# Second graph layer: message sums over five PSUM banks, and rows weighed by an SBUF copy of the weights

## What is computed

```python
    edge_index = jnp.stack([src, dst])
    x = _layernorm(x + _L0_gnn_ref(x, edge_index, L0_gnn_w0, L0_gnn_w1), axis=-1)
    x = _layernorm(x + _L1_gnn_ref(x, L1_gnn_W, L1_gnn_attn_src, L1_gnn_attn_dst, edge_index, edge_type_8), axis=-1)
```

```python
        h_src = h_all[edge_type, src]
        h_dst = h_all[edge_type, dst]
        scores = jnp.einsum('ehd,hd->eh', h_src, attn_src) + jnp.einsum('ehd,hd->eh', h_dst, attn_dst)
        scores = jnp.where(scores > 0, scores, NEG_SLOPE * scores)
        amax = jnp.maximum(jax.ops.segment_max(scores, dst, num_segments=n), 0.0)
        w = jnp.exp(scores - amax[dst])
        denom = jax.ops.segment_sum(w, dst, num_segments=n) + 1e-12
        w = w / denom[dst]
        msg = h_src * w[..., None]
        out = jax.ops.segment_sum(msg, dst, num_segments=n)
```

## Time and profile before

| What | us |
|---|---|
| Timed runs, median of 3 (lowest to highest) | 2754.34 (2751.61 to 2757.78) |
| Profiled execution: span from its first to its last instruction | 3067.8 |
| Busy in it: TensorE matmuls / weight loads | 2357.8 / 1676.6 |
| Busy in it: VectorE / ScalarE / POOL | 1943.7 / 1618.7 / 1840.7 |

### The profile page before, as it was taken

How to read it: one execution, slowest core, us unless ns; L and a number is a source line. 1 busy time by engine, 2 the same in 40 slices (tenths; PEclk the granted TensorE clock), 3 DMA queues, 4 the chain that set the end, 5 groups by cost and what they waited for, 6 DMA issues and landing times.

```text
span 3067.8 us, 38107 instructions
## 1 busy us (share of the span) xinstructions
PE 2357.8 (77%) x9936; PEld 1676.6 (55%) x9936; DVE 1943.7 (63%) x4273; ACT 1618.7 (53%) x3465; POOL 1840.7 (60%) x1875
## 2 busy tenths in 40 slices
PE   8786688899999989999981667766776667766675
PEld 3455566666666666666651545444554555554541
DVE  9893656554555555545530767767777777677787
ACT  4573455655555555555540555555655555455543
POOL 1004766677777767776617566666666666666625
PEclk9897899999999999999985777878878788687788
DMA  5103446644444444444533444444444444444424
GB/s 155 49 13 113 123 122 161 211 146 143 146 136 142 141 146 142 144 141 144 135 138 105 107 128 120 122 123 117 133 121 120 122 120 124 118 130 122 118 69 142
DMA packets 177777, 387.53 MB, mean 126 GB/s; under 512 B 42669, under 2 KB 106867, under 8 KB 171042
## 3 DMA queue, kind: packets, MB, share of 16 engines
q0 software_dynamic: 83888, 233.09, 28.3%
q1 hardware_dynamic: 86626, 99.05, 10.6%
q10 hardware_dynamic: 7056, 52.99, 4.5%
HBM read 302.96 MB, written 82.03 MB: 125 GB/s over the span
## 4 chain that ended last, share of the span: by engine, by line
PE 51%; DVE 18%; issue 15%; another core or an unknown queue 8%; ACT 3%; DVEq 2%; POOL 1%; DMA 1%; SPq 0%; ACTq 0%; POOLq 0%
PE ps L1695 22%; PE ps L1811 11%; PE ps L1745 10%; DVE nodes L895 6%; PE ps L1794 3%; DVE nodes L777 2%; DVE region L884 2%; PE ps L1664 1%; ACT region L1461 1%; PE ps L1652 1%; DVE edge_z L1029 1%; DVEq L895 1%; ACT region L1465 1%; DVE region L868 1%
## 5 line engine op out<-in xcount | busy, mean ns | idle before, releaser
L1303 POOL DMA_INDIRECT region<-y_d,edge_z x856 | 875.0, 1022 | 571.4 <-issue 231.4
L1348 POOL DMA_INDIRECT region<-ha_d,idx_t x880 | 891.7, 1013 | 495.3 <-issue 242.7
L777 DVE TENSOR_TENSOR nodes<-ps,nodes 128x512 f32 x856 | 591.8, 691 | 616.0 <-PE ps L1695 333.2
L1695 PE MATMUL ps<-region 128*128 128x256 f32 x3424 | 830.1, 394 | 134.7 <-issue 72.8
L1811 PE MATMUL ps<-region 128*128 128x264 f32 x1760 | 645.0, 502 | 279.5 <-DVE nodes L895 114.1
L1695 PEld LDWEIGHTS ps<-region 128*128 128x128 f32 x3424 | 654.2, 196 | 343.4 <-issue 207.3
L1811 PEld LDWEIGHTS ps<-region 128*128 128x128 f32 x1760 | 370.2, 237 | 467.1 <-issue 177.8
L895 DVE TENSOR_TENSOR nodes<-ps,nodes 128x264 f32 x880 | 374.0, 425 | 304.6 <-remote 207.1
L1461 ACT ACTIVATE region<-iota_n,edge_z 128x256 f32<-128x256 f32 x856 | 364.7, 500 | 62.7 <-PE ps L1695 40.3
L1745 PE MATMUL ps<-region,edge_z 128*128 128x512 f32 x784 | 366.8, 598 | 12.5 <-ACT edge_z L1491 7.5
L1503 ACT COPY region<-ps 128x512 f32<-128x512 f32 x196 | 114.2, 586 | 403.2 <-PE ps L1745 169.5
(11 more groups left out here) (265 smaller groups left out, 1826.8 us busy)
## 6 DMA issues: line engine op xcount, KB each, us to landing
ha_d<-region ACTq DMA_DIRECT2D x49, 1056.0 KB
region<-near_d SPq DMA_DIRECT2D x55, 512.0 KB
region<-ha_d,idx_t POOLq DMA_INDIRECT x880
region<-y_d,edge_z POOLq DMA_INDIRECT x856
edge_z<-level_d SPq DMA_DIRECT2D x55, 136.0 KB
kl_d<-region SPq DMA_DIRECT2D x8, 903.0 KB
edge_z<-kl_d SPq DMA_DIRECT2D x55, 129.0 KB
y_d<-edge_z SPq DMA_DIRECT2D x25, 256.0 KB, 3.2
```

Source lines behind the costliest of these rows:

```text
L777: v.tensor_tensor(into, ps[:, u, :], into, ALU.add).then_inc(added0, 1)
L1303: g.indirect_dma_start(rows0[c % RING][:, u, :], None, y_d, bass.IndirectOffsetOnAxis(ap=y_idx[:, k:k + 1], axis=0), bounds_check=node_bou ...
L1348: g.indirect_dma_start(rows[s][:, k, :], None, ha_rows, bass.IndirectOffsetOnAxis(ap=idx_t[:, B * b + k:B * b + k + 1], axis=0), bounds_ch ...
L1695: mm = t.matmul(ps[:, u, h * D:(h + 1) * D], lhsT=sel0[c % SEL][:, u, h * P:(h + 1) * P], rhs=rows0[c % RING][:, u, :], start=True, stop=True)
```

## The change

The sums of the second layer go round five banks, 0 to 4, by the step's number in the whole layer, so that a matmul waits for the add five steps earlier. Bank 4 is free for that since the turned weights now go to columns 128 to 255 of bank 7, beside the scores (columns 0 to 127) and the levels (256 to 511). As the banks must not be written by one engine while another reads them, the copy of the turned weights is made at once, before the factor's operand, and the transpose of the scores into bank 7 waits for it; on TensorE it now stands behind the last quarter of the sums of batch `i - 2`. The rows are multiplied by the copy in SBUF, which is in the last 8 columns of the same rows. The first sum of a batch no longer waits for the copy by a semaphore of its own. The factor row goes to the bank of the batch's first step.

```diff
+    SLOT = 5
...
-            w_turn = ps[:, 4, 0:P].rearrange("p (k h) -> p k h", k=B)
+            w_turn = ps[:, 7, P:2 * P].rearrange("p (k h) -> p k h", k=B)
 
             def weigh(b, q):
                 s = b % 4
                 if q == 0:
-                    v.wait_ge(w_turned, b + 1)
+                    v.wait_ge(w_ready, b + 1)
                 v.tensor_tensor(rows[s][:, 4 * q:4 * q + 4, 0:D].rearrange("p u (h d) -> p u h d", h=H),
                                 rows[s][:, 4 * q:4 * q + 4, 0:D].rearrange("p u (h d) -> p u h d", h=H),
-                                w_turn[:, 4 * q:4 * q + 4, :].unsqueeze(3).to_broadcast([P, 4, H, HD]),
+                                rows[s][:, 4 * q:4 * q + 4, D:AW].unsqueeze(3).to_broadcast([P, 4, H, HD]),
                                 ALU.mult).then_inc(msgs, 1)
...
-                v.tensor_tensor(acc[:, ds(tile * AW, AW)], ps[:, u, 0:AW], acc[:, ds(tile * AW, AW)],
+                v.tensor_tensor(acc[:, ds(tile * AW, AW)], ps[:, at % SLOT, 0:AW], acc[:, ds(tile * AW, AW)],
                                 ALU.add).then_inc(added, 1)
...
-                by = ps[:, 0, AW:AW + H]
+                by = ps[:, B * b % SLOT, AW:AW + H]
...
                 if a:
+                    v.wait_ge(w_turned, i)
+                    v.tensor_copy(rows[(i - 1) % 4][:, :, D:AW], w_turn).then_inc(w_ready, 1)
                     v.wait_ge(factors, i)
                     v.tensor_scalar(fm, factor, 1.0, ident[:, 0:1], ALU.subtract, ALU.mult).then_inc(fm_made, 1)
...
                 if a:
                     weigh(i - 1, 0)
-                    v.tensor_copy(rows[(i - 1) % 4][:, :, D:AW], w_turn).then_inc(w_ready, 1)
...
             def factor_rows(b):
                 t.wait_ge(fm_made, b + 1)
                 t.wait_ge(sel_made, 4 * b + 1)
-                t.wait_ge(added, B * b + 1)
-                t.matmul(ps[:, 0, AW:AW + H], lhsT=sel[0][:, 0, :], rhs=fm, start=True, stop=True).then_inc(fm_ps, 1)
+                if b:
+                    t.wait_ge(added, B * b - SLOT + 5)
+                t.matmul(ps[:, B * b % SLOT, AW:AW + H], lhsT=sel[0][:, 0, :], rhs=fm, start=True, stop=True).then_inc(fm_ps, 1)
 
             def sum_edges(b, q):
-                if q == 0:
-                    t.wait_ge(w_ready, b + 1)
                 t.wait_ge(msgs, 4 * b + q + 1)
                 t.wait_ge(sel_made, 4 * b + q + 1)
                 for u in range(4):
-                    t.wait_ge(added, B * b + 4 * q + u + 1)
-                    t.matmul(ps[:, u, 0:AW], lhsT=sel[q][:, u, :], rhs=rows[b % 4][:, 4 * q + u, :],
+                    at = B * b + 4 * q + u
+                    if at >= SLOT:
+                        t.wait_ge(added, at - SLOT + 5)
+                    t.matmul(ps[:, at % SLOT, 0:AW], lhsT=sel[q][:, u, :], rhs=rows[b % 4][:, 4 * q + u, :],
                              start=True, stop=True).then_inc(segs, 1)
...
                 if a:
                     t.wait_ge(exps, i)
-                    if i >= 2:
-                        t.wait_ge(msgs, 4 * i - 4)
-                    t.transpose(ps[:, 4, 0:P], e_row, ident[:, :]).then_inc(w_turned, 1)
+                    t.transpose(ps[:, 7, P:2 * P], e_row, ident[:, :]).then_inc(w_turned, 1)
+                if o:
+                    sum_edges(i - 2, 3)
                 if c:
                     t.wait_ge(zl_made, i + 1)
+                    if a:
+                        t.wait_ge(w_ready, i)
                     t.transpose(ps[:, 7, 0:P], z_c[h].rearrange("p k h -> p (k h)"), ident[:, :]).then_inc(turned, 1)
-                if o:
-                    sum_edges(i - 2, 3)
```

## The result

The changed kernel takes **2841.15 us** (median of 4 runs, 2839.61 to 2844.91), the kernel before 2756.06 us (2751.61 to 2759.17): a ratio of 1.0302, with a 95% interval from 1.0289 to 1.0316. That is 85 us slower, where 74 were forecast (2828 us, range 2742 to 2866).

A forecast was written before the change was run, and what follows sets the result against it. The prediction took POOL's gather queue to bound both layers; 82 us of held gathers less 8 us of idle time gave 74 us, so 2754.3 + 74 = 2828 us, range 2742 to 2866 us.

The forecast's parts named there:

- What bounds the kernel: In the timed runs, the gather queue on POOL sets the time of both layers.
- a floor of 2746.0 us: Gathers without waits, 1135.1 us (first layer) and 1168.9 us (second), plus 442.0 us outside the two stages.
- The 8 us to spare: Idle time left in POOL's queue: timed runs 8 us above the floor, subtracted from the holds' cost.
- the 82: Second-layer POOL time added by the holds: 206 weighings among the gathers at 0.396 us each, 82 us.
- The hold on a gather: A two-input instruction begun some 0.05 us before a second-layer gather's start holds it until 0.88 us after its own end.
- even phases: Mean taken over weighings and gather starts: 77% of weighings meet a start, at 0.513 us on average, 0.396 us each.
- Two inputs in SBUF hold a gather: Weighing with the SBUF copy makes VectorE contend with POOL's second-layer gathers and lengthen them: 82 us, bounds 0 and 211.
- SBUF no cheaper to read than PSUM: The weighing's second operand in SBUF makes the multiplication neither cheaper nor dearer: 0.
- The early copy and the moved transpose at nothing: Copy moved up on VectorE, scores' transpose moved back on TensorE: 0 each; the transpose up to 55 x 1 us without cover.
- Five banks at nothing: Fifth bank and dropped copy wait shrink TensorE's and VectorE's waits: 0 in the sum, at most 38.8 us gained.
- A sign that was wrong: The profiled span, where POOL had 175.2 us of waits, rises by less than the timed runs or not at all.

The follow-up runs named there:

- before again: The kernel before with no edit, run for a second profile: 2750.48 us measured, span 2748.7 us.
- the disturbed execution: The first profiled execution of the unchanged kernel before, which the forecast was read from: span 3067.8 us.
- rows twice: Against a control with 110 added instructions (one operand in PSUM, 2763.12 us), these read the rows twice, both inputs in SBUF: 2825.12 us, ratio 1.0252.

## Why the prediction was right

- **What bounds the kernel: right, by a sum whose errors cancel.** The forecast had POOL's queue set the time, with a floor of 2746.0 us. In before again the second layer takes 1161.2 us (floor 1168.9) and the first, from 245.9 to 1424.0 us, 1178.1 us (floor 1135.1); the rest is 2748.7 - 1161.2 - 1178.1 = 409.4 us (taken as 442.0 from the disturbed execution). The floor of the first layer had no place for 30 other instructions of POOL among the gathers, 23.8 us, nor for three waits for the sums near the start of the stage, 19.7 us; no other pause there is over 0.34 us. So the claim fits the trace of the first layer but for these three waits; no run took a gather away there. It is shown for the second, the only one that the change touches.
- **The 8 us to spare: wrong.** They were subtracted from the 82, and the second layer had none: POOL's pauses in before again are 0.3 us each, the same as after. That is most of the 11 us between 74 and 85.
- **The hold on a gather: right, its mean by luck.** It ends 0.88 us after the weighing, as read from an instruction of 0.29 us; for scans it is less, 0.82 us, and the scan of the earlier trace rows already showed 0.81. 87.1 us over the 212 weighings that fall among the gathers are 0.41 us each, against 0.396. But this was to come from even phases, 77% of the weighings at 0.513 us each. Counted in the trace, 194 of the 212 (92%) lengthen a gather, by 0.457 us on average, and not evenly: 78 by 0.1 to 0.3 us and 51 by 0.8 to 0.9. The two errors cancel; in rows twice, where the phases gathered at one place, they didn't. The count was 206 in the disturbed trace. The mean of L1350 rose by 0.10 us; 0.09 was named.
- **Two inputs in SBUF hold a gather: right.** What the traces show is above: a gather meets an instruction with two inputs in SBUF and is held, by up to a microsecond. That a shared port does it no run shows. The Trainium skill (SBUF — State Buffer, "Who interferes with whom") states the contention for GpSimd instructions that read SBUF; its inference that a tensor_tensor leaves descriptors alone doesn't hold for these gathers, which take 1.46 and 1.83 us across one.
- **SBUF no cheaper to read than PSUM: right.** 1210 ns from SBUF, 1205 from PSUM. The Trainium skill (Perfetto Trace Analysis, "Optimizing Scalar/DVE Operations") gives VectorE about 60 ns of overhead on SBUF and about 125 on PSUM; that difference doesn't show here, where one of two inputs moved.
- **The early copy and the moved transpose at nothing: right.** The copy (L956) has no wait ahead of it in 55 times, and the transpose of the scores (L1833) waits for it once, for 13.5 us. The kernel with the early copy and the new order, but not the operand, takes 2756.74 us.
- **Five banks at nothing: right.** VectorE's wait for the sums' matmuls was 12.0 us in before again, not the 38.8 of the earlier trace rows, and is 6.1 now. TensorE's wait for the copy has gone, as forecast, and its waits for the adds and for the weighing (221.1 and 70.9 us) are longer than what they replace (121.2 and 33.9). TensorE idles elsewhere.
- **A sign that was wrong:** the profiled span was to rise less than the timed runs, as POOL had 175.2 us of waits in it. It rests on the disturbed execution. Against before again the span rose by 89.1 us, where the timed runs rose by 85; against the 3067.8 us of the earlier trace rows it fell by 230.
- What stays open: the fifth bank with the weights read from PSUM wasn't tried, nor was the fifth bank by itself. With the weights read there, bank 7 would have to stay unwritten until the last weighing of a batch, which puts the next batch's transpose of the scores behind it.

## What to carry to other kernels

Find the queue that never waits: here its idle time is a pause of 0.30 us ahead of each gather, and when its gathers grow, the waits of the others for their landing grow as much. While such a queue issues gathers from POOL, keep one input of every long VectorE instruction in PSUM, even if a copy in SBUF is at hand; where both must be in SBUF, shorter instructions cost less (87, 40 and 23 us of gather time here for one, two and four). A mean over even phases is a guess: two queues can meet at the same place again and again, as 73 of 106 instructions did here. And check a floor against two executions: the one at hand was 319 us over another of the same kernel.

## What the runs showed of the hardware that was not expected

- A gather of 128 rows, 1.012 us when nothing meets it, took up to 2.066 us behind one multiplication of 1.21 us.
- The hold ends at a fixed distance behind the instruction's end: 0.88 us for multiplications of 0.41, 0.68 and 1.21 us alike, 0.82 us for scans of 0.43 and 0.47 us.
- Pieces without a gap sometimes hold as one: 1.70 us behind three adjoining pieces of 0.41 us, in 16 gathers of 173 that could have been held so.
- The two queues don't meet at even phases. In rows twice 73 of 106 instructions met the next gather's start at 0.4 to 0.6 us, and an instruction cost 0.59 us where even phases would have cost 0.4.
- One traced execution of the same kernel took 3067.8 us and another 2748.7 us. The waits of the first for the sums, most of them without a named release, were gone in the second.
